# Expert loops of a two-block vision model on one core: order of the last pair of tiles, a second result bank at the end, and turns of a constant before the first tile

## The reference

```python
# block 0: 4 experts, each token goes to the one with the highest gate
h = gelu(x @ w1[e] + b1[e]);  y = h @ w2[e] + b2[e]      # 192 -> 768 -> 192
# block 1: 8 experts, each token goes to its best two; results are weighted with top_p
top_p, top_i = top_k(softmax(x @ w_gate), 2);  top_p /= top_p.sum(-1)
y = sum_k top_p[k] * (gelu(x @ w_fc[top_i[k]]) @ w_proj[top_i[k]])
```

## Time and profile before

| what | value |
|---|---|
| time, median of 3 runs | 687.85 us (684.83 to 687.98) |
| time of the profiled execution | 689.49 us |
| its span, first to last instruction | 687.7 us |
| TensorE busy (matmuls) | 504.6 us, 73% |
| VectorE, ScalarE, GpSimd busy | 355.7, 160.8, 155.9 us |
| mean granted TensorE clock | 0.848 of full speed |
| chain that ended last: TensorE, VectorE, issue | 63%, 23%, 5% |

### The profile page before, as it was taken

The page is one execution under the profiler, slowest core; times in us unless marked ns, Lnnn a source line. Parts: engine busy times, 40 slices in busy tenths (PEclk is TensorE's granted clock), DMA queues, the critical chain, the costliest instruction groups (busy, mean ns, idle before and its releaser), DMA issues.

```text
span 687.7 us, 12923 instructions
## 1 busy us (share of the span) xinstructions
PE 504.6 (73%) x4632; PEld 450.5 (66%) x4633; DVE 355.7 (52%) x1087; ACT 160.8 (23%) x340; POOL 155.9 (23%) x156
## 2 busy tenths in 40 slices
PE   4999996998405407189999358741599999999950
PEld 4999996457404304079998356711499999999950
DVE  1599995365999896522221385858222222222206
ACT  4100001222793324023333031210021111111110
POOL 2794000000001000144422100000544444443220
PEclk9999998797656658579999759765699999999995
DMA  9960000000004002196659300200976666667116
GB/s 323 413 224 12 1 1 0 1 3 3 1 0 162 1 0 92 45 271 196 184 165 366 109 1 1 85 7 1 245 192 185 184 183 183 184 179 176 59 47 251
DMA packets 35239, 81.48 MB, mean 118 GB/s; under 512 B 6870, under 2 KB 17970, under 8 KB 34034
## 3 DMA queue, kind: packets, MB, share of 16 engines
q1 hardware_dynamic: 29618, 69.36, 31.5%
q0 software_dynamic: 5568, 11.41, 6.0%
HBM read 70.33 MB, written 10.42 MB: 117 GB/s over the span
## 4 chain that ended last, share of the span: by engine, by line
PE 63%; DVE 23%; issue 5%; ACT 4%; DMA 4%; SPq 1%; ACTq 0%; POOL 0%; DVEq 0%; POOLq 0%
PE ps L932 17%; PE ps L690 13%; PE ps L909 11%; PE ps L917 6%; DVE stat L1065 2%; PE ps L760 2%; PE ps L761 2%; DVE h L1616 2%; PE ps L900 1%; PE ps L788 1%; PE ps L665 1%; PE ps L874 1%; DMA arena<-tok_w 1%; DVE xT L1487 1%; PE ps L667 1%
## 5 line engine op out<-in xcount | busy, mean ns | idle before, releaser
L932 PE MATMUL ps<-arena,xn 128*128 x696 | 125.0, 330 | 5.1 <-ACT xn L601 2.6
L932 PEld LDWEIGHTS ps<-arena,xn 128*128 128x128 f32 x696 | 113.4, 192 | 6.5 <-issue 6.3
L690 PE MATMUL ps<-arena 128*128 128x192 f32 (+1 forms) x672 | 99.4, 335 | 9.2 <-DMA arena<-x_strips 9.0
L690 PEld LDWEIGHTS ps<-arena 128*128 128x128 f32 (+1 forms) x672 | 97.8, 196 | 10.0 <-ACT arena L452 8.6
L414 POOL DMA_INDIRECT xT<-rows,from_i x58 | 56.1, 967 | 184.8 <-DVE to_i L1521 165.3
L909 PE MATMUL ps<-xn,arena 128*128 128x128 f32 x696 | 91.5, 284 | 0.0
L426 POOL DMA_INDIRECT made<-xT,to_i x58 | 57.0, 983 | 149.2 <-DVE xT L1541 93.8
L909 PEld LDWEIGHTS ps<-xn,arena 128*128 128x128 f32 x696 | 88.0, 200 | 0.4
L1541 DVE COPY xT<-ps 128x192 f32<-128x192 f32 x39 | 13.9, 358 | 100.4 <-PE ps L932 100.4
L604 ACT ACTIVATE xn<-ps 128x384 f32<-128x384 f32 x78 | 32.0, 495 | 132.1 <-PE ps L919 132.1
L1529 DVE COPY xn<-ps 128x128 f32<-128x128 f32 x58 | 16.6, 287 | 61.3 <-PE ps L901 61.3
(11 more groups left out here) (337 smaller groups left out, 749.1 us busy)
## 6 DMA issues: line engine op xcount, KB each, us to landing
arena<-ffn_a SPq DMA_DIRECT2D x58, 384.0 KB, 3.5
arena<-ffn_b SPq DMA_DIRECT2D x116, 96.0 KB, 3.8
arena<-x_blocks SPq DMA_DIRECT2D x16, 384.0 KB, 7.0
arena<-x_strips SPq DMA_DIRECT2D x3, 1536.0 KB, 12.1
arena<-ffn SPq DMA_DIRECT2D x4, 1152.0 KB
rows<-xn SPq DMA_DIRECT2D x8, 384.0 KB, 2.5
xn<-made SPq DMA_DIRECT2D x8, 384.0 KB, 4.3
arena<-tok_w SPq DMA_DIRECT2D x8, 288.0 KB, 7.4
```

The source lines that it names most:

```text
L690: mm = pe.matmul(tok_ps(t), xs[rows, strip % GRID, 2 * j + b, 128 * c:128 * c + 128], wg[rows, w_chunk(P, b) + c, :], start=bank not in op ...
L932: mm = pe.matmul(ps[:, 7, 0:DIM], hT[:, u % 2, 128 * c:128 * c + 128], F["w2"][:, bass.ds(e2 + DIM * c, DIM)], start=(c == 0), stop=(c == ...
```

## The change

Three edits, all of them in both stages of experts.

1. In the last step of a stage (k = N - 3, for which tile k + 3 does not exist), `rest(k+2)`, the one of the last tile, comes right behind `up(k+2)` and so ahead of `down(k)` and `down(k+1)`. It is taken away behind the loop.
2. `down(N-2)` writes to bank 0 and its `result` reads it there; all others stay in bank 7. `down(N-2)` and `down(N-1)` wait for one result less in `y_out`: `down(N-2)` for that of tile N - 4, `down(N-1)` for that of tile N - 3.
3. After `tiles_ready` and ahead of `turn(0)`, TensorE transposes the constant into bank 3: 20 times in block 0 and 26 times in block 1.

```diff
+        def result_bank(k, tiles):
+            return 0 if isinstance(k, int) and k == tiles - 2 else 7
...
-            def keep_clock(count):
+            def keep_clock(count, bank=7):
                 for _ in range(count):
-                    pe.transpose(ps[:, 7, 0:128], ones, ident)
+                    pe.transpose(ps[:, bank, 0:128], ones, ident)
...
                 def down(k, u, e2):
+                    last = isinstance(k, int) and k >= N - 2
                     pe.wait_ge(sem(f"g_out{n}"), k + 1)
-                    at_least(pe, sem(f"y_out{n}"), k)
+                    at_least(pe, sem(f"y_out{n}"), k - last)
                     for c in range(HCH):
-                        mm = pe.matmul(ps[:, 7, 0:DIM], ...
+                        mm = pe.matmul(ps[:, result_bank(k, N), 0:DIM], ...
...
                     turn_of(4)
                     up_of(2)
+                    if not there(3):
+                        rest((u + 2) % 6)
                     turn_of(5)
                     down(k, u, e2)
...
                 pe.wait_ge(sem(f"tiles_ready{n}"), 1)
+                keep_clock(26 if n else 20, 3)
                 turn(0, 0, 0)
...
                 pairs_of(pe, N, step)
                 e2 = expert_of(N - 1)
-                rest((N - 1) % 6)
                 down(N - 1, (N - 1) % 6, e2)
...
-                        ins = dve.tensor_tensor(yo[:, u % 3], ps[:, 7, 0:DIM], b2_all[...], ALU.add)
+                        ins = dve.tensor_tensor(yo[:, u % 3], ps[:, result_bank(k, N), 0:DIM], b2_all[...], ALU.add)
                     else:
-                        ins = dve.tensor_copy(yo[:, u % 3], ps[:, 7, 0:DIM])
+                        ins = dve.tensor_copy(yo[:, u % 3], ps[:, result_bank(k, N), 0:DIM])
```

More of the change, by code:

```diff
@@ L927, in down @@
                 def down(k, u, e2):
+                    last = isinstance(k, int) and k >= N - 2
                     pe.wait_ge(sem(f"g_out{n}"), k + 1)
-                    at_least(pe, sem(f"y_out{n}"), k)
+                    at_least(pe, sem(f"y_out{n}"), k - last)
                     for c in range(HCH):
-                        mm = pe.matmul(ps[:, 7, 0:DIM], hT[:, u % 2, 128 * c:128 * c + 128], F["w2"][:, bass.ds(e2 + DIM * c, DIM)],
+                        mm = pe.matmul(ps[:, result_bank(k, N), 0:DIM], hT[:, u % 2, 128 * c:128 * c + 128], F["w2"][:, bass.ds(e2 + DIM * c, DIM)],
                                        start=(c == 0), stop=(c == HCH - 1))
@@ L1538, in result @@
                     if n == 0:
-                        ins = dve.tensor_tensor(yo[:, u % 3], ps[:, 7, 0:DIM], b2_all[:, bass.ds(e, DIM)], ALU.add)
+                        ins = dve.tensor_tensor(yo[:, u % 3], ps[:, result_bank(k, N), 0:DIM], b2_all[:, bass.ds(e, DIM)], ALU.add)
                     else:
-                        ins = dve.tensor_copy(yo[:, u % 3], ps[:, 7, 0:DIM])
+                        ins = dve.tensor_copy(yo[:, u % 3], ps[:, result_bank(k, N), 0:DIM])
                     ins.then_inc(sem(f"y_out{n}"), 1)
```

## The result

The changed kernel took 680.32 us (median of 6 runs, 679.28 to 681.88) against 687.91 us before (6 runs, 684.75 to 691.17): ratio 0.9896, 95% interval 0.9866 to 0.9925, so 5 to 9 us less. The forecast was 681.8 in a range of 679.0 to 684.8. The profiled execution took 679.28 us, its span is 677.5. It is the fastest of the six, and the profiled one of before (689.49) is 1.6 above the median, so the two profiles lie further apart than the medians.

A forecast was written before the change was run, and what follows sets the result against it. TensorE's matmuls bound the steady loop, so only stage ends and starts could gain. Ends of 4.54 + 1.89 = 6.43, taken as 5.75 for the unsafe clock, plus 0.25 for starts: 687.85 - 6.0 = 681.8 us, range 679.0 to 684.8.

The forecast's parts named there:

- What bounds: Steady loop of the experts: bound by TensorE's matmuls alone, 120.00 of 120 us busy, and untouched by the change.
- Block 0's end: Last tiles of block 0: the waits for copy and gelu and the slow last down go, saving 4.54 us.
- signs of being wrong: Named beforehand: a ScalarE wait ahead of the last down, a later first turn relative to L889, or readback taking the gain.
- the register load: ScalarE at block 0's end, after its wait with nothing covering it: between nothing and 0.4 us, taken as 0.2.
- Block 1's end: Last tiles of block 1: 7.33 us against 9.22 from the tail's start to the last copy, saving 1.89.
- The clock term: Block 0's last down at full clock: 1.68 us, absent if an execution's clock stays up; 1.0 was counted.
- The starts: Constant's turns hidden under the gather's wait raise the clock, lost again before up(0): 0 to 0.3 us, 0.25 counted.
- rival B: Starts: clock stays up through the gap, 1.2 to 3.9 us more, about 679.5; chance 0.17.
- C: Ends: last tile's gelu starts only behind the second down, saving just 1.6 to 3.3 us, 684.5 to 686.2; chance 0.08.
- D: Whole kernel: no measurable change, within 0.5% (3.4 us), the saved time waited out at the readback; chance 0.05.
- E: Starts: constant's turns don't overlap each other and outlast the rows' arrival, making it slower, 694 at 0.55 each; chance 0.03.

The follow-up runs named there:

- e1: The full change without the turns of the constant at the starts: 681.42 us against 686.62 for the kernel before, ratio 0.9918.
- e5: The full change with ScalarE's register load in block 0 moved ahead of its wait: 680.81 us against 687.17 for the kernel before, ratio 0.9903.
- e2: The kernel before with only the turns of the constant added at the starts: 686.10 us against 686.62, ratio 0.9989.
- e6: The full change with 40 and 27 constant turns, 7 more between the first two tile turns and 3 before up(0): 677.87 us, ratio 0.9869 to before.
- e7: The full change with 60 and 78 constant turns in place of 20 and 26, meant to outlast the gathers: 681.20 us, ratio 0.9904 to before.
- e10: The full change with ScalarE's early register load, weight loads of tiles 2 to 5 held back, and more turns bridging to up(0): ratio 0.9941 to before.
- e4: The kernel before with only the second result bank, the last rest left behind the loop: 683.34 us, ratio 0.9941.

## Why the prediction was right, point by point

**What bounds.** The steady loop did not move: from the first rest to the last tile's `up` it took 71.88 us in block 0 before and after, and 158.15 and 158.14 in block 1. All that was saved between the first rest and the last copy lies behind that `up`. And rest to last copy is the same 81.33 and 166.70 in the change and in e1, which differ at the starts alone.

**Block 0's end, 4.54 forecast, 3.96 measured.** The mechanism is that of the text, but one of its signs of being wrong came true: a wait on ScalarE is left ahead of the last down, above the 0.3 us that I allowed for a gap, and `rest` to the last copy took 7.92 us and not 7.4. The term that was mis-sized is the register load. I had bounded it above by 0.4 us and taken 0.2, so that it just hid behind `down(17)`. It left a wait of 0.53 us, and e5, which moves nothing else, gave 0.54 back. The rest nearly cancels: `rest` took 0.87 to the next work and not 0.77, it started 1.53 behind `up` where `down` had started 1.44 behind, and two downs in a row took 4.17 where I had 4.30.

**Block 1's end, 1.89 forecast, 2.11 measured.** Three downs in a row took 6.12 us; I had summed 2.15, 2.15 and 2.21. The 2.15 came from a row that has a small issue gap behind it, which a chain of downs does not have. `rest` to the last copy took 7.02 us where I had 7.3.

**The clock term.** 1.68 of the 6.43 I called unsafe to carry over. e2 shows it: the same wait, no fall. That the medians differ by 7.6 and not by less than 6 is therefore not evidence that it is always there; the parts that the profiles show are 6.1 at the ends with the fall, 4.4 without, and about 0.6 at the starts. The remainder is within the interval of the ratio, which reaches from 5 to 9 us; the fourth stretch, 1.4 us shorter at a higher clock, may be part of it. That the medians lie 7.6 apart where I had 6.0 is inside the range, but it is no evidence for each term.

**The starts, 0.25 forecast.** The steps came as told: the turns fit under the gather's wait, raise the clock, and it is lost again before `up(0)`. One size was off: with the clock rising on the way, 26 turns took 4.57 us and not 5.9, so that 2.71 us of the wait were left in block 1 and not 1.3. The Trainium skill ("TensorE: Matmul & The Clock Gate", section "Part 4: PE-mode transpose") says that transposes do not make TensorE count as busy for its clock. The profile after disagrees too: 20 and 26 turns of a constant took the clock to 1.00 while TensorE ran nothing else. What they bring was 0.9 in the one pair of profiles and 0.6 on average over eight; e2's 0.8 has zero in its interval. So that the third edit gains anything is not shown. The upper bound that I gave to rival B was wrong in its step: I let only one of two `up` hide behind the gathers in block 0. With the clock up throughout, e6 got 0.1 us there. The third tile's rows bind as the second's do. So B falls in block 0 for one reason more than the one I gave: not only is the clock lost, it is worth little at this place. In block 1, where I had put 2.7 us, no profile settles it: in e6 the clock fell before `up(0)`, in e7 the first tile was 2.7 us late, and in e10, where `up(0)` took 1.50 us, VectorE's next copy waited for "remote". An estimate comes from e7, which went from the second `turn` to the first rest in 3.69 us at the full clock, against 5.54 in the change: at most some 1.8 us, if the rows of the next tiles are in time, which no run shows.

**The rivals.** C is excluded by the timeline (the gelu starts behind the first down, 375.92). D is excluded by the time and by the readback, which is issued 2.98 us behind the last copy in both kernels (before: the earlier trace rows). E is excluded with a margin: 60 turns in 8.64 us are 0.144 each.

## What to carry to other kernels

Where a hand-written order has a loop and a tail, look at the tail for work that is ready earlier: the last tile's matmuls, behind two others, cost no more when moved ahead of them, and what waited for them on another engine then runs under those two. Remove both things that tie the tail together at once (here the order and the single bank): each alone uncovered the other's wait (0.31 and 0.90 us in block 1, 2.11 together). Before you pay for a fast clock at a start, look at whether what follows waits for a transfer.

## What the runs showed of the hardware that I had not expected

The register load behind ScalarE's wait cost about 0.54 us where nothing covered it (e5 against the change); ahead of the wait it cost nothing that shows.

The same idle time of 2 us did not always end in the same clock: 1.97 us ahead of the last down of block 0 brought it to 1.2 GHz in before, 1.96 us left it at 2.4 in e2, and 1.96 us let it fall in the middle of that down in e4. That makes 1.7 us between executions of the same code. In the unchanged fourth stretch 1.4 us go with the clock as well (0.70 against 0.77). In the first stretch, whose length differs by 2.2 us, no such link shows: the mean clock is 0.80 to 0.83 in the ten profiles, and the lowest, e4's, goes with 285.18 us while before, at 0.82, has 285.94.

In e7 the first tile was turned 2.7 us late because of the constant's turns, and only 0.3 us of that were left at the first rest: what came late waited for no rows, and ran at the full clock.
